# One exponential instruction over two heads' scores where their PSUM banks are neighbours

## The reference

```python
x = L0_attn_x                                       # (4, 1024, 512) fp32
x = x + 0.5 * ffn(layernorm(x))                     # 512x512 weights rounded to -1, 0, 1, times their mean
x = x + attn(layernorm(x))
x = x + 0.5 * ffn(layernorm(x))

def attn(x):                                        # 16 heads of 32
    kqv = (x @ Wqkv + bqkv).reshape(b, s, 3, 16, 32)
    q, k, v = kqv[:, :, 0], kqv[:, :, 1], kqv[:, :, 2]
    scores = einsum('bsnh,btnh->bnst', k, q) / sqrt(32)
    scores = triu(scores) - 10000 * tril(ones, -1)
    attn = softmax(scores, axis=2)
    return einsum('bnkq,bknh->bqnh', attn, v).reshape(b, s, 512) @ Wo + bo
```

## Time and profile before

| | us |
|---|---|
| three runs of the kernel | 1250.35, 1261.48, 1263.49 |
| their median | 1261.48 |
| the profiled execution's own time | 1254.48 |
| its span, first to last instruction | 1252.8 |
| granted TensorE clock, mean of the span | 0.959 of 2.4 GHz |

### The profile page before, as it was taken

The page is one execution under the profiler, slowest core; times in us unless marked ns, Lnnn a source line. Parts: engine busy times, 40 slices in busy tenths (PEclk is TensorE's granted clock), DMA queues, the critical chain, the costliest instruction groups (busy, mean ns, idle before and its releaser), DMA issues.

```text
span 1252.8 us, 26364 instructions
## 1 busy us (share of the span) xinstructions
PE 1142.1 (91%) x9466; PEld 720.7 (58%) x9466; DVE 718.0 (57%) x2228; ACT 946.8 (76%) x2699; POOL 499.1 (40%) x579
## 2 busy tenths in 40 slices
PE   4698999897899999997899999997999999998986
PEld 3465555454566666664566666664666666654454
DVE  6755435477635566677644665667643565654334
ACT  1248878886788888886788888887788888888641
POOL 4821120169601343559701343449801343500263
PEclk9888979899999999999899999999899999999799
DMA  7421211021111212321112211321111211100120
GB/s 251 143 93 52 103 52 36 19 70 52 36 36 68 71 35 70 120 70 44 44 36 69 69 36 56 108 95 44 43 37 59 80 36 53 44 10 3 36 68 34
DMA packets 41968, 77.71 MB, mean 62 GB/s; under 512 B 5488, under 2 KB 11632, under 8 KB 41840
## 3 DMA queue, kind: packets, MB, share of 16 engines
q1 hardware_dynamic: 41840, 76.04, 18.2%
HBM read 49.81 MB, written 25.17 MB: 60 GB/s over the span
## 4 chain that ended last, share of the span: by engine, by line
PE 66%; POOL 12%; ACT 11%; DVE 6%; issue 4%; DMA 1%; SPq 0%; ACTq 0%; POOLq 0%; DVEq 0%
PE bank L1055 26%; PE bank L1115 12%; PE bank L1145 9%; PE bank L1167 8%; ACT masked_scores L962 7%; PE bank L1080 6%; POOL hn L670 5%; POOL xt L680 3%; PE bank L1151 2%; PE bank L1072 2%; POOL rstd L660 2%; DVE masked_scores L816 1%; ACT prob L990 1%; DVE qT L792 1%; ACT qT L913 1%
## 5 line engine op out<-in xcount | busy, mean ns | idle before, releaser
L816 DVE CUSTOM_DVE_ANT_0 masked_scores<-bank,mask 128x512 f32<-128x512 f32 (+3 forms) x768 | 382.2, 554 | 287.9 <-PE bank L1115 250.0
L962 ACT ACTIVATE masked_scores<-masked_scores,mst 128x512 f32<-128x512 f32 (+3 forms) x768 | 462.9, 610 | 46.8 <-DVE mst L816 46.3
L990 ACT ACTIVATE prob<-bank 128x512 f32<-128x512 f32 (+3 forms) x768 | 312.8, 493 | 51.3 <-PE bank L1151 49.9
L714 POOL TENSOR_SCALAR_AFFINE_SELECT prob<-prob 128x512 f32<-128x512 f32 x128 | 81.5, 636 | 478.0 <-ACT prob L990 477.4
L1115 PE MATMUL bank<-kT,qT 32*128 32x512 f32 (+2 forms) x2304 | 198.1, 395 | 27.4 <-DVE qT L792 13.4
L1115 PEld LDWEIGHTS bank<-kT,qT 32*128 32x128 f32 x2304 | 112.3, 187 | 167.0 <-issue 83.3
L1055 PE MATMUL bank<-hT,wqk 128*128 128x512 f32 x768 | 198.2, 408 | 0.0
L1145 PE MATMUL bank<-qT,kT 32*128 32x512 f32 (+2 forms) x2304 | 185.0, 389 | 5.2 <-DVE mst L816 4.0
L1055 PEld LDWEIGHTS bank<-hT,wqk 128*128 128x128 f32 x768 | 143.7, 194 | 36.4 <-ACT prob L990 5.7
L670 POOL TENSOR_SCALAR hn<-xt,mv,rstd 128x512 f32<-128x512 f32 x76 | 157.8, 2079 | 0.7 <-POOL rstd L660 0.5
L1145 PEld LDWEIGHTS bank<-qT,kT 32*128 32x128 f32 x2304 | 104.8, 188 | 83.2 <-issue 59.8
(11 more groups left out here) (88 smaller groups left out, 1066.0 us busy)
## 6 DMA issues: line engine op xcount, KB each, us to landing
wqk<-weight_scratch SPq DMA_DIRECT2D x30, 512.0 KB, 3.3
wvo<-weight_scratch SPq DMA_DIRECT2D x20, 512.0 KB, 5.9
xt<-in_L_attn_x_dram SPq DMA_DIRECT2D x32, 256.0 KB, 3.6
residual_scratch<-xt SPq DMA_DIRECT2D x32, 256.0 KB, 2.0
xt<-residual_scratch SPq DMA_DIRECT2D x32, 256.0 KB, 2.7
out_dram<-xt SPq DMA_DIRECT2D x32, 256.0 KB, 2.0
o<-in_L_attn_Wqkv_dram SPq DMA_DIRECT2D x12, 256.0 KB, 4.4
weight_scratch<-o SPq DMA_DIRECT2D x6, 512.0 KB, 2.9
```

Source lines behind the costliest of these rows:

```text
L714: nc.gpsimd.affine_select(out=part, in_=part, compare_op=ALU.is_ge, fill=0.0, base=0, pattern=[[0, 4], [1, P]], channel_multiplier=-1).the ...
L816: nc.vector.tensor_tensor_reduce(masked_scores[:, h, 0:n], psum(u, h)[:, 0:n], mask[:, off:off + n], -SCALE, BIG, ALU.add, ALU.min, mst[:, ...
L962: nc.scalar.activation(of, of, ACT.Exp, bias=mst[:, c + kc, at:at + 1], scale=-1.0, accum_out=ssum[:, c + kc, at:at + 1]).then_inc(a_free, 1)
L990: nc.scalar.activation(prob[:, at % 2, h, off:CW], psum(("S", b, n), h)[:, off:CW], ACT.Exp, scale=SCALE)\
```

## The change

`exponentials` used to issue one activation a head. Now it issues one for two neighbouring heads whenever their banks have neighbouring numbers, and adds 2 to `s_exp` when that instruction is done. For this the eight banks become one PSUM tensor, of which `bank[n]` is a slice; their order and size stay.

```diff
-        bank = [ctx.enter_context(nc.psum_tensor(f"bank{n}", [P, CW], F32)) for n in range(8)]
+        banks = ctx.enter_context(nc.psum_tensor("banks", [P, 8, CW], F32))
+        bank = [banks[:, n, :] for n in range(8)]
...
+        def pairs(u):
+
+            runs, h = [], 0
+            while h < 4:
+                n = 2 if h < 3 and BANKS.of[u][h + 1] == BANKS.of[u][h] + 1 else 1
+                runs.append((h, n, banks[:, BANKS.of[u][h]:BANKS.of[u][h] + n, :]))
+                h += n
+            return runs
...
             def exponentials(b, n):
                 off = step_of(n % STEPS)[2]
                 at = step(b, n)
-                for h in range(4):
-                    nc.scalar.activation(prob[:, at % 2, h, off:CW], psum(("S", b, n), h)[:, off:CW], ACT.Exp, scale=SCALE)\
-                        .then_inc(s_exp, 1)
+                for h, m, of in pairs(("S", b, n)):
+                    nc.scalar.activation(prob[:, at % 2, h:h + m, off:CW], of[:, :, off:CW], ACT.Exp, scale=SCALE)\
+                        .then_inc(s_exp, m)
```

More of the change, by code:

```diff
@@ L396, in psum @@
         def psum(u, i=0):
-            return bank[BANKS.of[u][i]][:, :]
+            return bank[BANKS.of[u][i]]
+        def pairs(u):
[5 more added lines that the diff above has]
+            return runs
         def split(u):
@@ L950, in evacuate @@
                 act.wait_ge(value_done, step(b, g * STEPS + (STEPS if c else QPC)))
-                nc.scalar.activation(chunk(b, CHUNKS * g + c), accv[:, :], ACT.Identity).then_inc(accv_free, 1)
+                nc.scalar.activation(chunk(b, CHUNKS * g + c), accv, ACT.Identity).then_inc(accv_free, 1)
             def block_sums(u):
```

## The result

| | before | with the change |
|---|---|---|
| runs | 1250.35 to 1263.49, 4 runs | 1288.0 to 1292.52, 4 runs |
| median, us | 1256.28 | 1290.14 |
| ratio | | 1.0267, 95% interval [1.0195, 1.034] |
| span of the profiled execution | 1252.8 | 1286.2 |
| its mean granted clock | 0.959 | 0.939 |

The change makes the kernel 2.7% slower. The forecast was 1276 us, 1.2% slower, with a range that ended at 1290. The direction and the mechanism hold; the size is off by more than a factor of two (34 us against 15), and the median lies 0.14 us above the upper edge of the range. Of the kernel before, one run made later beside the last three experiments (1297.15 us at a mean clock of 0.822) was in a slower state and stands in no comparison.

A forecast was written before the change was run, and what follows sets the result against it. PE's queue was taken as the bound in two stretches, POOL in three others. Terms +25 + 1 - 5 - 4 - 2 = +15 us on the 1261.5 us median gave 1276.5, rounded to 1276, 1.2% slower; range 1256 to 1290.

The forecast's parts named there:

- What bounds the kernel: PE's queue bounds 328 to 540 and 606 to 825 us; POOL sets the pace in three stretches, 209 us, 19%.
- Part 1, ACT's saving: 331 merged exponentials save 0.06 us each, 20 us of ACT's 947, worth about 2 us at the end.
- Part 2, head 0: Head 0's bank comes back 0.43 us later at 512 columns; A's fourth head waits for it, 25 us in all.
- i = 0 and 4: 31 steps where PV is only 128 columns wide: A pays the full 0.43 us, 11.2 us.
- i = 5 to 8: 60 steps with PV of 512 columns: 17 pay 0.43 us (6.1 us), 43 pay 0.19 (6.9 us).
- Part 2, heads 1 and 2: Transposes and projections waiting for these heads' banks: between 6 us lost and 8 gained, taken as +1.
- Part 3, what is absorbed: Waits PE has anyway swallow part of the delay: 5 us in POOL's stretches, 4 us where ACT is late.
- the delay that reaches DVE's maxima: DVE's maximum starts when A ends, so it and ACT's sums come later; runs beside PE's delay, charged nothing.
- Covered: Rival: PE's later waits take up most, a third of the 15 us is left: 1266 us, chance 0.27.
- faster: Rival: ACT was the bound, its 0.06 us a merge shortens the loop by 13 us: 1248 us, chance 0.10.
- Everything carries: Rival: delay returns through DVE and ACT's sums, nothing absorbed, head 2 costs 6 us: +31, 1292 us, chance 0.08.
- The signs: Pair 1.0 to 1.05 us; ACT down 20; A's waits over 90, 45 us; i = 6 A 1.16; PE share lower.

The follow-up runs named there:

- the last three experiments: By order of the text: the change without pairs in the last group (1.0234), without pairs in the last batch (1.0207); kernel before with 0+1 paired in i = 1, 2, 3 (0.9982).
- the late release without merging: Kernel before with single exponentials, but where the change has a pair only the second adds to the semaphore, and it adds 2: 1292.03 us, ratio 1.0239.
- 2+3 alone: The changed kernel with only heads 2 and 3 paired, heads 0 and 1 single: ratio 1.0071 against the kernel before, +11 us at equal clock.

## Why the prediction was half right

*What bounds the kernel.* Right. Each of PE's stretches loses 0.14 to 0.16 us a step, each of POOL's 0.04 to 0.08.

*Part 1, ACT's saving.* The merge was sized right: 1.018 us for a pair, and 20.9 us less in the exponentials' groups. ACT as a whole was relieved of 13.5 us and not of 20. That this is worth 2 us at the end is neither shown nor refuted.

*Part 2, head 0.* The mechanism is shown by the late release without merging. For i = 0 and 4 the 11.2 us came as 11.9. For i = 5 to 8 the 13 us came as 10.5 with pairs there alone, and as 7.6 in the change: the pairs in i = 0 and 4 take 2.8 off these gaps. Two errors nearly cancelled in the 13. The prediction let 17 of the 60 blocks stand for head 0 before; in the trace 7 do, for more than 0.2 us. And with the change most of the others (36 of the 60) stand 0.24 to 0.27 us, not 0.19: 7 x 0.84 x 0.43 + 53 x 0.84 x 0.24 is 13 again. The narrow steps brought 0.5 where 1 stood. In all 25 us became 20.

*Part 2, heads 1 and 2.* +1 stands against +3, the change's 24 less the 21 of heads 0 and 1 alone. That lies within the bounds (-8 to +6), which do not hold for 2+3 alone (+11), where A has not been held up.

*Part 3, what is absorbed.* Here the sum failed. The 4 us for waits that PE has anyway are near the 5 that A's gaps fell short of 25; part of that is luck, since 2.5 of the 5 are the size of i = 5 to 8. The 5 us for POOL's stretches were too many: the three lost 2.4 us where the rate of PE's stretches would have given 5.3, so they took back 3. Term by term: 15 - 1 (A) + 2 (POOL) + 2 (heads 1 and 2) = 18, and 20 if ACT's saving is worth nothing. 24 is measured at equal clock, with 2 to 3 us of doubt in the correction.

The rest has a candidate in a term that the prediction put at nothing: the delay that reaches DVE's maxima. PE's scores mostly take banks that a block A held, and wait for its maximum. Before, and then after:

```profile
PEld bank L1145 <- DVE mst L816: 10.4, 19, 1.2
...
PE bank L1145 <- DVE mst L816: 4.0, 9, 0.6
```

```profile
PEld banks L1155 <- DVE mst L826: 17.7, 30, 1.2
...
PE banks L1155 <- DVE mst L826: 6.1, 12, 0.8
```

That is 9.4 us more, on the engine that bounds the run, and the late release without merging has the same 23.8 us. ACT's wait for these maxima rose too, from 46.3 us in 70 slots to 69.7 in 87. Against it, the waits of projections, transposes and scores for exponentials fell from 41.7 to 31.7 us: that is cover behind A. How much of each reaches the end of the run stays open.

*The clock.* I named a lower granted clock in the PE stretches as a cost not charged. It stayed at 1.00 there, and fell at the two ends of the run, most of which the earlier trace rows leaves out. That is the other 6 to 10 us. The low level was in the trace of before, too (0.82 from 217 to 255 us); a range that adds these us at its upper edge would have reached to 1300.

*The rivals.* "Covered" and "faster" fell. "Everything carries" (1292) has the right time, but 6 to 10 us of that are the clock, which it doesn't have. Of its two parts, no absorption is wrong at A, behind A and in POOL's stretches, and the feedback over DVE's maxima shows in the rows above, which no experiment isolated.

*The signs.* The pair's time and the 47.7 us of waits came as said. A's waits became 85 and not over 90, ACT's saving was smaller, the i = 6 block took 1.21 us and not 1.16, PE's share did not fall, and POOL's stretches changed a little.

## What to carry to other kernels

An instruction that serves two buffers releases both at its end; before merging, look up who takes the first buffer next, and how long after its release. If that is the engine that bounds the run, the merge costs up to the difference between the late release and the slack, in every round, whatever it saves on the engine that merges. Read the slack by kinds of steps and not as a mean: here 31 of 182 blocks had none, and they paid 11.9 of the 20 us.

## What the runs showed of the hardware

A ScalarE activation over two neighbouring PSUM banks takes 1.018 us for 1,024 columns, where one of 512 takes 0.599; back to back the merge saves 0.06 us. The Trainium skill (ScalarE: Activation LUTs, What ACT_TABLE_LOAD costs) has 186 ns plus 0.833 ns a column with 93 ns of overlap, which makes by estimate 1.039 us for the pair, 2% above the trace. The 93 ns that a merge would save by it (186 less 93) are more than the 63 ns that the trace gives (20.9 us over 331 merges).

Not expected was how much of the scatter of this kernel is TensorE's clock. In one set of twelve runs of the kernel before, the one with the highest mean clock (0.963) took 1250.88 us and the one with the lowest (0.938) 1265.69. It isn't the whole of it: in another set a run at 0.912 took only 1253.88 us.
